# Generated-parameter attention: parameters made a stage earlier, two normalisations fused, later sequences normalised inside the loop

## The reference

```python
x = x + _L1_attn_ref(_layernorm(x), ...)      # stage 2: 16 heads of 8, causal softmax
x = x + _L1_ffn_ref(_layernorm(x), ...)       # stage 3
x = x + _L2_attn_ref(_layernorm(x), ...)      # stage 4

def _gen_param(sub, Wl, W, Bp):
    p = jnp.einsum('a...,a->...', sub, Wl[0])         # a of 2: two "subs", mixed
    return jnp.tanh(p) * W + Bp
def _block(hs, ln1_g, ln1_b, ...):                    # hs is already layer-normed once
    h = _layernorm(hs, ln1_g, ln1_b)
    q, k, v = jnp.split(_student_linear(h, *ca), 3, axis=-1)
    scores = where(causal, q k^T / sqrt(8), -10000)
    o = softmax(scores) v
    hs = hs + _student_linear(o, *cp)
    m = _student_linear(_gelu_new(_student_linear(_layernorm(hs, ln2_g, ln2_b), *cf)), *cm)
    return hs + m
```

## Time and profile before

| | |
|---|---|
| median of 3 runs | 1720.01 us (1719.81 to 1721.59) |
| the profiled execution | 1717.78 us, of which the span of its instructions is 1715.7 us |
| busy | PE 81%, DVE 63%, ACT 44%, POOL 43% of the span |
| mean granted clock of PE | 0.882 of full speed |
| stage 2, from the first instruction of DVE to that of stage 3 | 342.6 to 564.8 us |
| stage 3 | 564.8 to 659.4 us |
| stage 4, attention | 659.4 to 895.7 us |

### The profile page before, as it was taken

How to read it: one execution, slowest core, us unless ns; L and a number is a source line. 1 busy time by engine, 2 the same in 40 slices (tenths; PEclk the granted TensorE clock), 3 DMA queues, 4 the chain that set the end, 5 groups by cost and what they waited for, 6 DMA issues and landing times. The chain is left out here.

```text
span 1715.7 us, 24915 instructions
## 1 busy us (share of the span) xinstructions
PE 1390.8 (81%) x8900; PEld 844.5 (49%) x8907; DVE 1088.0 (63%) x2898; ACT 748.9 (44%) x1168; POOL 740.5 (43%) x795
## 2 busy tenths in 40 slices
PE   4586578879998793899978899799999999985193
PEld 2354556554444462444435677554555545534062
DVE  6766588667886547688843332578778777756212
ACT  3554244325666143366644333355455454430040
POOL 4442345442223545422233543255546465563533
PEclk9688689958999796599988999999999999996597
DMA  2000005020000124000001020000000000003213
GB/s 92 11 7 2 33 1 210 0 84 1 2 1 1 49 63 173 1 2 1 2 1 46 7 99 1 1 1 1 1 1 1 1 1 1 1 1 123 62 52 97
DMA packets 29562, 52.74 MB, mean 31 GB/s; under 512 B 3216, under 2 KB 24592, under 8 KB 27264
## 3 DMA queue, kind: packets, MB, share of 16 engines
q1 hardware_dynamic: 26144, 44.36, 7.3%
q0 software_dynamic: 3296, 6.78, 1.2%
HBM read 29.07 MB, written 21.02 MB: 29 GB/s over the span
## 5 line engine op out<-in xcount | busy, mean ns | idle before, releaser
L2392 DVE CUSTOM_DVE_ANT_0 s_masked_scores<-s_for_max,s_mask_qk 128x128 bf16<-128x128 f32 (+3 forms) x512 | 227.2, 487 | 59.9 <-PE s_for_max L2216 58.1
L2825 POOL TENSOR_TENSOR wbuf<-s_probs 128x1024 f32<-128x1024 f32 x64 | 151.9, 2374 | 205.3 <-ACT s_probs L2984 205.3
L2984 ACT ACTIVATE s_probs<-s_scores 128x1024 f32<-128x1024 f32 x128 | 132.2, 1033 | 201.7 <-PE s_scores L2906 201.7
L2168 POOL TENSOR_SCALAR_AFFINE_SELECT s_probs<-s_probs 128x256 f32<-128x256 f32 x256 | 100.9, 407 | 271.4 <-ACT s_probs L2323 157.3
L3026 DVE TENSOR_REDUCE s_negmax<-s_for_max 128x2 f32<-128x1024 f32 x126 | 152.2, 1208 | 20.0 <-PE s_for_max L2881 20.0
L2216 PE MATMUL s_for_max<-s_k_stack,s_q_stack 32*128 32x128 f32 (+3 forms) x512 | 142.7, 443 | 27.2 <-DVE s_max_wide L2392 17.5
L3033 DVE RECIPROCAL s_recip<-s_pv_and_sums 128x128 f32<-128x128 f32 x128 | 116.7, 934 | 47.3 <-PE s_pv_and_sums L2932 47.3
L2216 PEld LDWEIGHTS s_for_max<-s_k_stack,s_q_stack 32*128 32x128 f32 x512 | 72.3, 206 | 129.6 <-DVE s_max_wide L2392 89.1
L2323 ACT ACTIVATE s_probs<-s_scores 128x1024 f32<-128x1024 f32 x128 | 127.3, 1024 | 18.2 <-PE s_scores L2237 18.0
L2919 PE MATMUL s_pv_and_sums<-s_probs,s_v 128*64 128x512 f32 x512 | 123.9, 605 | 0.9 <-DVE wbuf L3041 0.9
L2251 PE MATMUL s_pv<-s_probs,s_v_and_one 128*32 128x512 f32 (+3 forms) x1024 | 95.0, 465 | 1.5 <-DVE s_o L2411 1.5
(11 more groups left out here) (574 smaller groups left out, 3449.8 us busy)
## 6 DMA issues: line engine op xcount, KB each, us to landing
rows_by_expert<-s_empty_rows SPq DMA_DIRECT2D x8, 1032.0 KB, 10.4
s_w<-extra SPq DMA_DIRECT2D x2, 2048.0 KB, 9.8
wbuf<-w SPq DMA_DIRECT2D x1, 3460.0 KB, 11.2
s_probs<-extra SPq DMA_DIRECT2D x1, 2898.0 KB, 10.1
wbuf<-w SPq DMA_DIRECT2D x1, 2888.0 KB, 14.1
wbuf<-w SPq DMA_DIRECT2D x1, 2124.0 KB, 7.9
dispatched<-s_empty_slots SPq DMA_DIRECT2D x1, 2064.0 KB, 8.5
s_rows<-dispatched SPq DMA_DIRECT2D x8, 258.0 KB, 2.7
```

The source lines that it names most:

```text
L2168: last = nc.gpsimd.affine_select(out=diag, in_=diag, compare_op=ALU.is_ge, fill=0.0, base=0, pattern=[[0, diag.shape[1]], [1, P]], channel ...
L2392: last = nc.vector.tensor_tensor_reduce(out=junk[:, m % 2, at:at + n], in0=p1[m % 2][:, at:at + n], in1=mask[:, S - n:S], scale=1.0, scala ...
L2825: nc.gpsimd.tensor_tensor(added[half], probs[:, g % 2, 2 * half, :, :], probs[:, g % 2, 2 * half + 1, :, :], ALU.add).then_inc(s_added, 1)
L2984: nc.scalar.activation(probs[:, g % 2, j, :, :], p2[:, :, :], ACT.Exp, scale=dh ** -0.5).then_inc(s_exp, 1)
```

## The change

The generated parameters of stage 4 are made in stage 3. SP loads `extra` there; ACT mixes the subs after the shared part of sequence 0 and of sequence 1, and takes both tanh after that of sequence 2; DVE adds the subs and finishes the first 520 columns; POOL finishes the other 1412 after its last scatter; ACT makes the stacked hi parts at its end, DVE the lo parts just before its last sums.

The two norms of stage 4 become one from x: POOL's factor is now var x (1 + eps) + eps^2 in place of var + eps. The tensor hs itself, still needed for the residual, is made by POOL, a sequence at a time (`make_hs`).

In both attention stages only sequence 0 is normed ahead of the plan, and sequence 1 has its statistics there. The plan gets items "stats", "scaled" and "ln" (transposes and copies) for the later ones, and "ln" uses the bank `odd_jobs`. POOL's parts (the differences `lo`, the reciprocal roots, the residual bias) stand between the quads. The turned o gets a tile of its own.

```diff
@@ LayerNorm.rstd_of
+        if self.twice:
+            nc.gpsimd.tensor_scalar(self.rstd[:, ts], self.mv[:, ts, 1], 1.0 + LN_EPS, LN_EPS * LN_EPS,
+                                    ALU.mult, ALU.add).then_inc(self.s_eps, 1)
@@ sorted_ffn: sync
             sh.load_next(sp, stage)
+            sp.dma_start(generators[:, :], sh.extra[nxt]).then_inc(s_extra, 16)
@@ sorted_ffn: gpsimd, last
+            other = sub0[:, halves[1]]
+            pool.wait_ge(s_tanh, 2)
+            nc.gpsimd.tensor_tensor(other, other, g_scale[:, halves[1]], ALU.mult).then_inc(s_others, 1)
+            pool.wait_ge(s_others, 1)
+            nc.gpsimd.tensor_tensor(other, other, g_bias[:, halves[1]], ALU.add).then_inc(s_others, 1)
@@ sorted_ffn: scalar
             for c in range(EARLY):
                 for f in range(n_sh):
                     shared_silu(c, f)
+                if c < 2:
+                    mix(range(c * n_seg // 2, (c + 1) * n_seg // 2))
+            bend(0)
+            bend(1)
...
+            for k in range(2):
+                nc.scalar.copy(wst[0][:, k, :, 0:3, :], three_times(k)).then_inc(s_whi, 1)
@@ sorted_ffn: vector
             for c in range(EARLY):
                 if c + 1 < EARLY:
                     for f in range(n_sh):
                         shared_hidden(c + 1, f)
+                if c < 2:
+                    add_subs(c)
                 add_shared(c)
+            near = sub0[:, halves[0]]
+            dve.wait_ge(s_tanh, 1)
+            nc.vector.tensor_tensor(near, near, g_scale[:, halves[0]], ALU.mult).then_inc(s_gen, 1)
+            dve.wait_ge(s_gen, 1)
+            nc.vector.tensor_tensor(near, near, g_bias[:, halves[0]], ALU.add).then_inc(s_gen, 1)
...
             add_shared(B - 1)
+            for k in range(2):
+                dve.wait_ge(s_whi, k + 1)
+                nc.vector.tensor_tensor(wst[1][:, k, :, 0:3, :], three_times(k),
+                                        wst[0][:, k, :, 0:3, :].bitcast(F32), ALU.subtract).then_inc(s_wlo, 1)
@@ causal_plan
+    behind(("q_stack", 0), ("scaled", 1))
+    for c in range(1, B):
+        q = QUADS * c
+        if c >= 2:
+            behind(("max", q - 5, 3), ("stats", c))
+            behind(("max", q - 4, 5), ("scaled", c))
+        behind(("max", q - 2, 3), ("ln", c))
@@ causal_attention: gpsimd
         nc.gpsimd.iota(row[:, :], pattern=[[0, 1]], base=0, channel_multiplier=1).then_inc(s_row, 1)
+        clear_gpsimd(pool)
+        ln.rstd_of(pool, 0)
         nc.gpsimd.memset(mask[:, :], 0.0).then_inc(s_mask, 1)
         nc.gpsimd.memset(wide[:, :, :, :, :], 0.0).then_inc(s_wide, 1)
...
-        norm_gpsimd(pool)
-        pool.wait_ge(ln.s_xn, NT)
+        ln.rstd_of(pool, 1)
         nc.gpsimd.memset(v32[:, :, :, :, HD8:32], 0.0).then_inc(s_ones, 1)
@@ causal_attention: gpsimd, after the six cuts of quad q
+            c = q // QUADS + 1
+            if c < B and q % QUADS == 0:
+                ln.low_part_by(nc.gpsimd, pool, c)
+            if c + 1 < B and q % QUADS == 1:
+                ln.rstd_of(pool, c + 1)
+            if c < B and q % QUADS == 2:
+                add_bias(c)
@@ causal_attention: tensor, scalar
+            elif item[0] == "ln":
+                odd_bank(item)
+                ln.turned(pe, item[1], pm)
...
+            elif item[0] == "ln":
+                ln.copied(act, item[1], pm[:, :])
@@ causal_attention: vector
+        ln.stats_of(dve, 0)
...
+        ln.scaled(dve, 0)
...
         before_vector(dve)
+        ln.low_part(dve, 0)
+        ln.stats_of(dve, 1)
@@ low_rank_attention: tensor
-            ln.tensor(pe)
+                if h == 10:
+                    ln.turned(pe, 0)
@@ generated_attention
+        def make_hs(pool, c):
+            ts = slice(c * TPC, (c + 1) * TPC)
+            pool.wait_ge(ln.s_mv, (c + 1) * TPC)
+            nc.gpsimd.tensor_scalar(rstd[:, ts], ln.mv[:, ts, 1], LN_EPS, 1.0, ALU.add, ALU.mult).then_inc(s_once, 1)
...
+            for t in range(c * TPC, (c + 1) * TPC):
+                nc.gpsimd.tensor_scalar(sh.hs[:, t, :], sh.x[:, t, :], ln.mv[:, t, 0:1], rstd[:, t:t + 1],
+                                        ALU.subtract, ALU.mult).then_inc(s_hs, 1)
```

More of the change, by code:

```diff
@@ L1450, in sorted_ffn @@
     J, WIDE, RING = SORT_TILES, 3 * f_exp, 6
+    nxt = stage + 1
+    g_width, n_seg = sum(n for _, n in L2_SEGMENTS), len(L2_SEGMENTS)
+    first_half = sum(n for _, n in L2_SEGMENTS[:2])
+    halves = [slice(0, first_half), slice(first_half, g_width)]
+    g_w, gen = sh.w(nxt), sh.gen(sh.w(nxt))
+    sub0 = g_w["sub0"]
+    sh.until_generated = ExitStack()
+    wst = sh.w_stacked = [sh.until_generated.enter_context(nc.sbuf_tensor(f"s{nxt}_w_stacked_{m}", [P, 2, H8, 4, HD8], F32R))
+                          for m in ("hi", "lo")]
     EARLY = B - 1
@@ L1548, in _ @@
             ln.rstd_of(pool, 3)
+            for half in wst:
+                nc.gpsimd.memset(half[:, :, :, 3, :].bitcast(F32), 0.0).then_inc(s_zero, 1)
             pool.wait_ge(sh.fields_cleared, 16 * SORT_CLEARS)
@@ L1701, in _, with mix, bend @@
                 ln.copied(act, c)
+            def mix(segments):
+                for k in segments:
+                    at, m = sum(n for _, n in L2_SEGMENTS[:k]), L2_SEGMENTS[k][1]
+                    for i, sub in enumerate((sub0, sub1)):
+                        nc.scalar.activation(sub[:, at:at + m], sub[:, at:at + m], ACT.Identity,
+                                             scale=g_w["a"][:, 2 * k + i:2 * k + i + 1]).then_inc(s_mix, 1)
+            def bend(half):
+                act.wait_ge(s_mixed, half + 1)
+                nc.scalar.activation(sub0[:, halves[half]], sub0[:, halves[half]], ACT.Tanh).then_inc(s_tanh, 1)
+            act.wait_ge(sh.wsem[nxt], 16)
+            act.wait_ge(s_extra, 16)
             for c in range(EARLY):
@@ L2147, in _, with add_bias @@
         nc.gpsimd.memset(v32[:, :, :, :, HD8:HD8 + 1], 1.0).then_inc(s_ones, 1)
-        after_norm_gpsimd(pool)
+        pool.wait_ge(sh.wsem[stage], 16)
         resid = sh.x if hs is None else hs
-        for c in range(B):
+        def add_bias(c):
+            if make_hs:
+                make_hs(pool, c)
+            else:
+                pool.wait_ge(ln.s_xn, (c + 1) * TPC)
             ts = slice(c * TPC, (c + 1) * TPC)
@@ L2489, in generated_attention @@
     nc, w, tag = sh.nc, sh.w(stage), f"s{stage}"
-    width = sum(n for _, n in L2_SEGMENTS)
     with ExitStack() as ctx:
```

169 lines of the change are left out of this document (52 added, 117 removed).

## The result

The changed kernel takes 1727.78 us (median of five, 1725.06 to 1731.0), the kernel before 1720.01: ratio 1.0039, 95% interval 1.0021 to 1.0058. It is slower by 7.8 us in the medians and by 7.3 between the profiled executions (1725.06 with a span of 1723.2, against 1717.78 with 1715.7). Forecast were 1723.9 and +3.9, range 1713 to 1730; the result lies on the side that I called slower, the likeliest of the three.

The account below looks back on a forecast made before the run. PE idles ahead of the plans; inside them PE and DVE are nearly full. Stage 2 +6.1 and stages 3 and 4 -2.2 gave +3.9 us: 1721.7 profiled, 1723.9 median, range 1713 to 1730.

Parts of the forecast that it names:

- the side that I called slower: Whole kernel: a median slower than 1723.4 us, given a chance of 0.46.
- Stage 2's start and stage 4's start: Ahead of both plans: first score product 1.1 us earlier in stage 2, 10.3 earlier in stage 4 with 3.8 already paid.
- The holds by POOL's clearing: Ahead of the plans: DVE's scalings wait while POOL clears tiles, 1.3 us for the first, 0.8 for sequence 1's.
- 8 to 12 us nearer: Stage 4's start: first projection this much nearer to the stage's first DVE instruction than the 22.0 us before.
- ln in the plan: Attention steps: v waits behind ln's transposes and copies in the one bank; +5.0 us in stage 2, +5.9 in stage 4.
- Statistics and scalings: In both plans: four more DVE stretches per stage for sequences 2 and 3, 0.55 us each, +2.2 per stage.
- the term most mis-sized: Stage 2 in all: -1.1 at its start, +5.0 for ln, +2.2 for statistics and scalings, together +6.1 us.
- Stage 3: Making the parameters there: +1.9 us at the start, +1.0 for DVE's lo parts, +0.95 held by POOL; +3.8 in all.
- The later norms hide: In the plans: each ln costs only its transposes, 0.55 us, and DVE's pieces nothing; 1711.9 us, chance 0.18.
- Stage 3 gives nothing away: Stage 3: scalings fit ACT's gaps, lo parts fit DVE's wait, taking 2.8 us off; 1721.1 us, chance 0.18.
- The clock suffers as well: Steps with v: PE's new waits lower its clock for a while, 0.9 us per ln, +5.4; 1729.3 us, chance 0.14.

Follow-up runs that it names:

- e3: Changed kernel with POOL clearing the mask, wide tile and v's tile only after the scalings, in both stages; ratio 0.9995 to the kernel before.
- e2: Changed kernel with each later sequence's ln (transposes, two copies) one step earlier in the plan; ratio 1.0006 to the kernel before.
- e6: e2 with one exponential put ahead of ln's copies in ACT's list, for sequences 2 and 3; ratio 0.9949 to the kernel before.
- e4: Changed kernel with all four sequences of stage 4 normalised ahead of its plan; ratio 0.9966 to the kernel before.
- e7: Changed kernel with ACT's stage 3 waits behind sequence 0's first gates and POOL's two sums among its scatters; ratio 1.0036 to the kernel before.
- e9: Changed kernel, stage 3: ACT's waits behind the first gates, second eight scalings and DVE's sum behind sequence 2's gates; ratio 1.0014 to the kernel before.
- e10: Changed kernel with the edits of e3, e6 and e9 together; ratio 0.9921 to the kernel before, median 1706.6 us.
- e11: Changed kernel with stage 2 as before, stage 4's norms ahead of its plan, and e9's stage 3 edits; ratio 0.9949 to the kernel before, median 1707.1 us.

## Why the prediction was right, and where its sizes were off

The sign, the stage of each loss and gain, and in stages 2 and 4 the chain behind them came out; the whole was 3.4 us too small between the profiled executions. In stage 3 the size at the start came out by another path than the one forecast, which is luck. Point by point:

**Stage 2's start and stage 4's start.** Forecast were -1.1 and, with stage 3's cost, -10.3. Measured from each stage's own start: the score product 19.01 to 17.83 (-1.2), and 29.77 to 14.40 (-15.4, where 15.6 us were forecast in place of 14.4, so 1.2 better). The holds by POOL's clearing were real but mis-sized: the first took 0.8 in place of 1.3, the second 2.1 and 1.2 in place of 0.8. e3 shows that the second is mostly covered by ACT's low rows, so sizing it by its length would have been wrong in the other direction. The sign "8 to 12 us nearer" did not fit the sum, whose own terms give 14.0 (22.0 less 8.0); measured are 14.4.

**ln in the plan**, forecast +2.2, +1.4, +1.4 in stage 2 and +2.5, +1.7, +1.7 in stage 4. Measured on the steps: +2.28, +1.48, +1.49; +2.65, +1.86, +2.23, the last partly at a granted clock of 0.95. Right in size and in its wait, v behind ACT's second copy. The sentence beside it, that ACT waits at ln "holding two exponentials, but is done with them before PE asks for the buffers", is true only while PE waits for v: e2 shows PE waiting 0.88 us for one of them in a step without v, and e6, against e2, that this order too must be changed to get the time back.

**Statistics and scalings**, forecast 0.55 each. Measured 1.33, 0.44, 0.70 and 0.43 in stage 4, 1.25, 0.42 and 0.70 in stage 2, where the fourth lies in a step with a fallen clock: 2.9 per stage in place of 2.2. The first statistics fall into a step in which the clock is still rising, 0.86 in place of 0.96.

**Stage 2 is the term most mis-sized**, +9.2 for +6.1. 0.6 is the statistics. Some 2 us are clock: the drain, from the last maxima's transposes to stage 3, took 21.6 us at a mean clock of 0.82 in place of 19.4 at 0.97:

```profile
553.72:575.32 21.60, 16.37 (x138) 8.44 (x136) 3.02 (x8) 9.33 (x13) 4.99 (x15) 0.82 0.00 1
```

The same code in e4 and e7 drained in 19.4 and 19.3, so this is the execution and not the edit. What is left is the 0.3 by which the three ln were larger.

**Stage 3**, forecast +1.9 at the start and +1.95 at the end. At the end the mechanism is right and the size near: lo parts 1.79 us, of which 0.77 hold (0.95 forecast), and from the last scatter to the stage's end 11.0 us in place of 9.6, +1.4. The Trainium skill (SBUF — State Buffer, "Who interferes with whom") says that a DVE instruction with two SBUF inputs is locked out while GpSimd runs one that reads SBUF, and the trace agrees: the lo parts took 1.79 us where e7, with POOL done, took 1.02, and in e7's loop 3.01 stood for 0.15. The start cost 2.7 (first scatter at 52.08 in place of 49.36). PE's last shared product began 2.1 later (1.9 forecast), but the path to it was not the one I had. The second eight scalings did not hold back the gates of sequence 2; ACT stood idle behind them, for PE, and PE for DVE's products of sequence 1:

```profile
609.51 1.19 PE L1626 MATMUL s_ps_gate_up<-xnT,wbuf 128*128 128x512 f32 x1 [4.14 <-DVE s_shared_hidden L1822]
...
612.93 0.60 ACT L1722 ACTIVATE s_shared_silu<-s_ps_gate_up 128x512 f32<-128x512 f32 x1 [3.52 <-PE s_ps_gate_up L1626]
```

DVE made these late since its last part of the routing began 2.0 us later than before (29.55 into the stage in place of 27.58), behind the 3.84 us gap shown with e9. ACT's waits ahead of the gates exposed the table load, which I had at nothing, 1.3 us at the first gate, though e7 won nothing at the first scatter by hiding it. The sum of 1412 columns took 1.62 (1.6 forecast) and stood on the path as said: PE waited 1.85 us for the add behind it. The last 0.6 is clock: PE's last shared products took 2.86 us at a mean granted clock of 0.67, in place of 2.02 at 1.00.

**Before stage 2** the changed kernel was 1.35 us later in code that nobody edited. Over the eleven experiments that point lies between 342.0 and 347.4 (342.0 to 345.4 on the first chip, 345.2 to 347.1 on the second, 346.4 to 347.4 on the third), so part of any difference here is not the edit's. Averaging stages over the profiles that share their code, whatever the chip, gives stage 2 +7.3 (mean of four against four), stage 3 +4.3 (eight profiles) and stage 4 -6.6 (four): +5.0 in all, near the forecast +3.9. The remaining 2 to 3 us of the measured difference lie ahead of stage 2 or in the clock; with one profile of the kernel before, whether the program's layout or chance made them stays open. The ratios of e3 and e7 (0.9995 and 1.0036, the latter with a stage 3 that is 4.3 us longer) suggest that the 1.0039 itself is on the high side.

**The rivals.** "The later norms hide" had the price of ln right, 0.55 each (0.48 in e6), and the kernel wrong: for ln it becomes true with two edits of order, while statistics and scalings cost 0.3 to 1.3 each even then (e6). "Stage 3 gives nothing away" was right that the scalings fit into ACT's gaps, and fell by the sum, the lo parts and a later routing. "The clock suffers as well" is half true: dips came in steps 8 and 9 of stage 2 (11.57 and 11.05 us), in e2 for two whole steps, but equal code also ran without those in steps 8 and 9 (e4, e7), and the kernel before has its own.

## What to carry to other kernels

Work that stood where the critical engine idled costs little there, even at half clock; before moving it into a loop in which two engines are nine tenths busy, price it at what the loop's step grows by, not at what it takes off the start. When a wait goes and nothing comes back, look for a second queue behind the same producer: undo both before giving the theory up. When an edit gives more than it can explain, find out where along the stage the surplus comes; here most of e9's came ahead of the edited place. And compare stage lengths of profiles only with a profile of the same chip beside them. A wait instruction put into an engine's list can also hold back what came free with the next instruction: here ACT's table load.

## What the runs showed of the hardware

- A DVE minimum over one column with two SBUF inputs took 3.01 us in place of 0.15 while a POOL operation on 1412 columns, 3.17 us, ran (e7); with two of these among its scatters the loop was 4.5 us longer.
- Four DVE scalings from one SBUF tile were held as well, by POOL's memset, which reads nothing: 2.27 us in place of 1.10 in stage 4 (3.23 in stage 2, where a POOL sum held the last one too). The same section of the Trainium skill says that such an instruction can run in a mode that takes the pair of ports shared with GpSimd; the trace shows the hold and its end with the memset, not the mode.
- PE's granted clock fell to 1.2 GHz for some 13 us in stage 2 of e2 (0.75 and 0.77 over its two windows), with no idle time of PE above 0.52 us in the 7 us before. The rise in the first steps also moved between executions of one code: step 2 of stage 4 took 17.26 us in the changed kernel and 15.90 in e7.
- Gaps that no engine's work ends stood in stage 3 of every kernel but e9, e10 and e11, up to 6.52 us long; those three ran on a chip of their own, and what makes the gaps is not shown.
